# Seven chained products for the hidden layer, spread around the residual units, and one masking operation for two

## The reference

```python
h = jnp.maximum(_layernorm(x, axis=-1), 0.0)
x = x + _L0_gnn_ref(h, adj, adj, L0_gnn_W1, L0_gnn_W2, L0_gnn_W3)
h = jnp.maximum(_layernorm(x, axis=-1), 0.0)
x = x + _L1_gnn_ref(h, adj, L1_gnn_W1, L1_gnn_b1, L1_gnn_W2, L1_gnn_b2)
```

## Time and profile before

| | |
|---|---|
| median of 3 runs | 2262.76 us (2262.43 to 2263.21) |
| profiled execution | 2262.78 us, its span 2261.1 us |
| PE matmul busy | 2238.3 us, 99% |
| DVE busy | 1932.7 us, 85% |
| ACT busy | 1151.1 us, 51% |
| POOL busy | 1159.6 us, 51% |
| granted TensorE clock | 1.00 |

### The profile page before, as it was taken

One profiled execution on the slowest core, in us unless ns is written; L12 is line 12 of the kernel. 1 busy time (PEld: TensorE's weight loads), 2 busy tenths in 40 slices (PEclk: granted clock), 3 DMA queues, 4 the chain that ended last, 5 costly groups with the idle time before them and its releaser, 6 DMA issues.

```text
span 2261.1 us, 47549 instructions
## 1 busy us (share of the span) xinstructions
PE 2238.3 (99%) x12586; PEld 1905.3 (84%) x12586; DVE 1932.7 (85%) x10818; ACT 1151.1 (51%) x2901; POOL 1159.6 (51%) x1889
## 2 busy tenths in 40 slices
PE   8999999999999999999999999999999999999999
PEld 5777888888888888888888888888888888889998
DVE  7999999999888888888777778989999997547776
ACT  5555555555555555555555544444444444344554
POOL 6455555545555555555555557544555554343332
PEclk9999999999999999999999999999999999999999
DMA  3000000000000000000000000000000001024443
GB/s 105 29 29 29 16 24 29 29 29 20 29 29 29 29 29 19 19 28 28 28 28 28 28 29 20 29 29 19 24 25 28 28 28 38 19 80 132 135 132 107
DMA packets 90031, 90.14 MB, mean 40 GB/s; under 512 B 5376, under 2 KB 89088, under 8 KB 89856
## 3 DMA queue, kind: packets, MB, share of 16 engines
q1 hardware_dynamic: 89856, 88.23, 12.2%
HBM read 54.66 MB, written 33.55 MB: 39 GB/s over the span
## 4 chain that ended last, share of the span: by engine, by line
PE 91%; DVE 7%; ACT 1%; issue 1%; POOL 0%; DVEq 0%; ACTq 0%; POOLq 0%
PE ps L1550 74%; PE ps L1740 10%; PE ps L1472 3%; PE ps L1750 1%; DVE A L961 1%; PE ps L1683 1%; DVE A L965 1%; ACT squares L709 1%; DVE prods L998 1%; DVE xrow_sb L970 1%; ACT root_s L711 0%; DVE ps L1013 0%; DVE sc L979 0%; DVE sc L982 0%; DVE qcol L984 0%
## 5 line engine op out<-in xcount | busy, mean ns | idle before, releaser
L501 POOL COPY Eb<-sc 128x1 f32<-128x1 f32 (+1 forms) x254 | 46.7, 184 | 451.6 <-DVE v L986 231.9
L1550 PE MATMUL ps<-agg2T,w 128*128 128x256 f32 x1024 | 239.2, 379 | 0.0
L1550 PE MATMUL ps<-hid2T,xin 128*128 128x256 f32 x1024 | 236.1, 379 | 0.7 <-ACT h2T L754 0.7
L1550 PE MATMUL ps<-weightT,hid 128*128 128x256 f32 x1024 | 236.7, 379 | 0.0
L1550 PE MATMUL ps<-w,aggT 128*128 128x512 f32 x512 | 231.7, 592 | 0.0
L1550 PEld LDWEIGHTS ps<-weightT,hid 128*128 128x128 f32 x1024 | 189.5, 191 | 36.7 <-issue 14.3
L1550 PEld LDWEIGHTS ps<-hid2T,xin 128*128 128x128 f32 x1024 | 189.0, 190 | 26.2 <-ACT h2T L754 1.1
L1550 PEld LDWEIGHTS ps<-agg2T,w 128*128 128x128 f32 x1024 | 188.5, 190 | 25.3
L754 ACT ACTIVATE hid2T<-ps 128x512 f32<-128x512 f32 x256 | 151.0, 590 | 94.9 <-PE ps L1550 92.9
L1166 DVE SCALAR_TENSOR_TENSOR ahead<-ps,ne,ahead 128x14 f32<-128x14 f32 (+1 forms) x1020 | 189.9, 228 | 0.0
L1163 DVE RECIPROCAL ps<-ahead 128x14 f32<-128x14 f32 (+1 forms) x1024 | 188.3, 230 | 0.1
(11 more groups left out here) (387 smaller groups left out, 6194.3 us busy)
## 6 DMA issues: line engine op xcount, KB each, us to landing
xl<-in_x_dram SPq DMA_DIRECT2D x64, 256.0 KB, 2.8
xr<-in_x_dram SPq DMA_DIRECT2D x64, 256.0 KB, 2.8
x_dram<-xr SPq DMA_DIRECT2D x64, 256.0 KB, 2.3
xin<-x_dram SPq DMA_DIRECT2D x64, 256.0 KB, 2.8
out_dram<-xin SPq DMA_DIRECT2D x64, 256.0 KB, 2.2
w<-in_L_gnn_W_dram SPq DMA_DIRECT2D x1, 2048.0 KB, 10.3
w<-in_L_gnn_W_dram SPq DMA_DIRECT2D x1, 1024.0 KB, 12.2
w<-in_L_gnn_W_dram SPq DMA_DIRECT2D x1, 512.0 KB, 5.2
```

The lines of the kernel that those rows point to most:

```text
L501: pool.tensor_copy(Eb[:, bass.ds(k, 1)], sc[:, 4:5])
L1550: ins = pe.matmul(dst, a, b, start=start, stop=stop, skip_group_check=plan_.units[i][0][0] in "PG")
```

## The change

The hidden layer is computed as seven products of 256-column blocks, H1 to H7, the two items of a pair being the two block rows: seven units of two matmuls instead of four units of two matmuls of 512 columns. They are made for the NEXT pair at the end of the list: H1 H5 H2 H6, res 0, H7 H3, res 1, H4. H6, H7 and H4 accumulate in the bank of H1, H3 in that of H5; the banks come from a table (`bank_of`), and a unit waits for the last eviction of its own bank (`emptied`). POOL makes four sums of the aggregated nodes (`sum_of_nodes`) and three additions of products (`add_hid`); ACT evicts seven blocks and applies three ReLUs (`finish_hid`). The second aggregation now takes its blocks in the order (0,0) (1,1) (0,1) (1,0), each waiting for its own ReLU, and all four W2 sums on POOL wait for the last of them. `add_x` moves from the end of a round to step 1 of the next. The first pair keeps the old form, inside its first step. In householder_two the mask is applied to both blocks by one operation that reads a copy of `below` in PSUM (`under`), and the row's head is no longer cleared; ACT's squares start one column later instead.

```diff
         def columns(k0):
 
-            return max(k0, P) if k0 + 1 >= P else k0
+            return max(k0, P) if k0 + 1 >= P else k0 + 1
...
-        def plan(next_agg):
-            units = [("hid", j, q) for j in range(2) for q in range(NB)]
-            units += [("agg2", j, q) for q in range(H1B // 2) for j in range(2)]
+        def plan(next_pair):
+            units = [("agg2", 0, 0), ("agg2", 1, 1), ("agg2", 0, 1), ("agg2", 1, 0)]
             units += [(p, half, 0) for p in ("P1", "P5", "P6", "P3", "P7", "P2", "P4") for half in range(2)]
-            units += [("agg", j, 0) for j in range(2)] * next_agg
+            units += [("agg", j, 0) for j in range(2)] * next_pair
             units += [(p, m, 0) for p in ("G1", "G2", "G6", "G5", "G7", "G3", "G4") for m in range(NB)]
-            units += [("res", j, 0) for j in range(2)]
+            units += [("H1", 0, 0), ("H5", 0, 0), ("H2", 0, 0), ("H6", 0, 0)] * next_pair + [("res", 0, 0)]
+            units += [("H7", 0, 0), ("H3", 0, 0)] * next_pair + [("res", 1, 0)] + [("H4", 0, 0)] * next_pair
...
+        BANK_OF = {"H1": 1, "H5": 3, "H2": 0, "H6": 1, "H7": 1, "H3": 3, "H4": 1, "agg": 1}
...
+        HID_ADDS = (("C11", "H1", "H2"), ("C22", "H5", "H7"), ("C12", "H6", "H3"))
...
+            def sum_of_nodes(pair, n):
+
+                a11, a12, a21, a22 = (aggT[:, j, f, :] for j in range(2) for f in range(2))
+                a, b, op = {1: (a21, a22, ALU.add), 2: (node_block(1), a11, ALU.subtract), 3: (a11, a21, ALU.subtract),
+                            4: (a12, node_block(2), ALU.subtract)}[n]
+                if n == 1:
+                    pool.wait_ge(evac, before(pair - 1) + FULL.at["agg", 1, 0] + 3)
+                if n in (2, 4):
+                    pool.wait_ge(node_sum, 4 * pair + n - 1)
+                pool.tensor_tensor(node_block(n), a, b, op).then_inc(node_sum, 1)
+
+            def add_hid(pair, n):
+
+                name, other, block_ = HID_ADDS[n]
+                pool.wait_ge(evac, before(pair - 1) + FULL.at[block_, 0, 0] + 3)
+                pool.tensor_tensor(hid_block(name), hid_kept(other), hid_block(name), ALU.add).then_inc(hid_added, 1)
...
-                pool.wait_ge(evac, before(pair) + FULL.at["agg2", 1, 0 if n == 1 else 1] + 3)
+                pool.wait_ge(evac, before(pair) + FULL.at["agg2", 1, 0] + 3)
...
+                    if s == 1 and not (isinstance(t, int) and t == 0):
+                        for j in range(2):
+                            add_x(t - 1, j)
                     for kind, n in pool_turns[s]:
                         in_turn(t, kind, n)
-                for j in range(2):
-                    add_x(t, j)
...
+            def finish_hid(pair, n):
+
+                act.wait_ge(hid_added, len(HID_ADDS) * (pair - 1) + n + 1)
+                block_ = hid_block(HID_ADDS[n][0])
+                act.activation(block_, block_, ACT.Relu).then_inc(hid_fin, 1)
...
                 dve.wait_ge(col_ready, k + 2)
-                for b in range(NB):
-                    ins = dve.tensor_scalar(x_next[:, b:b + 1], col[:, b:b + 1], below[:, b, here:here + 1], None, ALU.mult)
-                at(ins)
-                at(dve.memset(head, 0.0), HOUSE - 20)
+                at(dve.tensor_tensor(x_next, col[:, :], under[:, :, here], ALU.mult), HOUSE - 19)
...
+                pe.wait_ge(evac, 8 if first_hid else before(pair) + emptied(plan_, i) + 3)
+                if stage in ("H5", "H6", "H7", "H3"):
+                    pe.wait_ge(node_sum, 4 * (pair + 1) + {"H5": 1, "H6": 2, "H7": 3, "H3": 4}[stage])
+                if (stage, j, q) == ("agg2", 1, 0) and not first_hid:
+                    pe.wait_ge(evac, before(pair - 1) + FULL.at["H4", 0, 0] + 3)
+                elif stage == "agg2" and not first_hid:
+                    pe.wait_ge(hid_fin, len(HID_ADDS) * (pair - 1) + {(0, 0): 1, (1, 1): 2, (0, 1): 3}[j, q])
```

More of the change, by code:

```diff
@@ L410, in placed @@
             return early, late, pool_turns
-        for first, last, steps, _ in GROUPS:
-            assert last - first == 1 or steps % 2 == 0
+        for (first, last, steps, _), k0 in zip(GROUPS, FIRST_STEP):
+            assert last - first == 1 or steps % 2 == 0 and k0 + 1 >= P
         @block.sync
@@ L592, in in_turn @@
                     sum_of_moving(pair, n)
+                elif kind == "hid":
+                    add_hid(pair + 1, n)
+                elif kind == "nodes":
+                    sum_of_nodes(pair + 1, n)
                 elif kind == "add":
@@ L633, in _ @@
                 keep_reflector(k, NB - 1)
+            for j in range(2):
+                add_x(WITH_STEPS - 1, j)
             pool.memset(halves[:, :, :], 0.0).then_inc(halved, 1)
@@ L690, in ln2_scalars, with pair_sums @@
                 pool.tensor_tensor(rs[:, s, 3, :], rs[:, s, 2, :], coef[:, 3, :], ALU.mult).then_inc(ln2_p, 1)
-            for s in range(2):
-                ln2_scalars(0, s)
+            def pair_sums(pair, more, plan_=FULL):
+                for n in range(1, 5):
+                    sum_of_moving(pair, n)
+                if more:
+                    for j in range(2):
+                        ln_minus_mean(pair + 1, j)
+                    for j in range(2):
+                        ln_scale(pair + 1, j)
+                for kind, n in POOL_ORDER[4:]:
+                    if more or kind not in ("nodes", "hid"):
+                        in_turn(pair, kind, n, plan_)
+                    if not more and (kind, n) == ("left", len(LEFTS) - 1):
+                        for s in range(2):
+                            ln2_scalars(0, s)
+            with pool.Fori(WITH_STEPS, PAIRS - 1) as t:
+                pair_sums(t, True)
+                for j in range(2):
+                    add_x(t, j)
             pair_sums(PAIRS - 1, False, ENDING)
@@ L764, in event @@
                     evacuate(pair, n)
+                elif kind == "hidfin":
+                    finish_hid(pair + 1, n)
                 else:
@@ L783, in act_steps @@
                     step_root(first_step + s, columns(k0 + s))
+                    if isinstance(t, int) and t == 0 and s == 0:
+                        for n, (j, q) in enumerate(FIRST_HID):
+                            act.wait_ge(unit, 2 + n + 1)
+                            act.activation(hid[:, j, q, :], ring[bank_of(("hid", j, q))][:, :], ACT.Relu).then_inc(evac, 1)
                     for kind, n in early_events[s]:
@@ L846, in pair_body @@
                         finish(pair, n)
+                    if more and (stage, j) in HID_AFTER:
+                        finish_hid(pair + 1, HID_AFTER[stage, j])
                     if more and (stage, j) == ("P2", 1):
@@ L851, in pair_body @@
                         act.activation(nrm[:, 1, :], nrm[:, 0, :], ACT.Sqrt).then_inc(z_root, 1)
-                    if not more and (stage, j, q) == ("agg2", 1, 1):
+                    if not more and (stage, j) == ("G5", 1):
                         normalise(0, 0)
```

157 lines of the change are left out of this document (101 added, 56 removed).

## The result

The changed kernel takes **2305.7 us** (median of 4 runs, 2304.96 to 2305.95) against 2262.6 before (4 runs beside them): 1.019 times as long, 95% interval 1.0177 to 1.0204, or 43 us slower.

The account below looks back on a forecast made before the run. PE, busy for 99% of the span, was taken to bound the kernel. Terms -25.8 - 6 + 30 + 10.5 + 14.5 + 2 = +25 us on 2262.76 gave 2288 us, range 2258 to 2305.

Parts of the forecast that it names:

- PE's own work: Matmuls of a pair: 28 records of 256 columns replace sixteen of 512, 0.83 us less for 31 pairs; -25.8 us.
- the rule of the narrow matmuls: Skill's issue gaps, estimated 98 ns for 256 columns, would make the change +66 us instead of -25.8; 2380 us, chance 0.01.
- The masking: DVE's Householder steps: one operation replaces two and a memset, 0.17 us off a late step; -6 us.
- POOL, added to and reordered: Step 2 of a round: PE waits for POOL's first sum, 1.7 us in early and 1.05 in 12-step rounds; +30 us.
- LayerNorm of the next pair: In 11-step rounds PE's aggregation waits for ACT's late LayerNorm output, 0.95 us for 11 rounds; +10.5 us.
- The end of a round on ACT: ACT's evictions and ReLUs delay the next round's root, so PE waits for q 0.9 or 0.5 us; +14.5 us.
- The rest: Rounds without steps: ACT and POOL wait for nothing of DVE, and evictions have time to spare; 0 us.
- The tail: Last pair: normalisation now stands behind one eviction and holds later ones; +2 us (0 to 4).
- rival 1 or 2: 1: everything hides as planned, 2233 us, chance 0.10; 2: only part of the waits comes true, 2262 us, chance 0.06.
- Rival 3: POOL, late by four sums in step 1, is late again, another 0.7 us in 22 rounds; 2303 us, chance 0.07.
- Rival 4: DVE is held by POOL's added operations, 4.4 us in each of 22 rounds; 2385 us, chance 0.01.

Follow-up runs that it names:

- the mended kernel: Changed kernel with five edits of order on POOL and ACT, plus first-round sums of weights ahead of LayerNorm's mean; 2229.2 us, 0.985 of the kernel before.
- LayerNorm one step earlier: Changed kernel with LayerNorm of the next pair placed one step earlier (LN_AT 0 and 1 in place of 1 and 2); 2285.2 us.
- Round 0: Changed kernel, first round only: POOL makes all eight weight sums in step 0, w3 sums in steps 2 and 3, w1 sums in step 6; 2300.3 us.

## Why the prediction was right or wrong

The sum came out 18 us too low (+25 against +43). Of that 10.9 us are the first round without steps, 5.0 are q in step 5, 4.3 are q in round 0, 2.4 and 2.1 the waits for POOL's sum and for LayerNorm, which were a little longer than forecast; against it stand 6.0 at the end of a round, which was forecast too long, and about 1 of all else. Without that error in the other direction the forecast would have been 24 us too low.

- **PE's own work**, -25.8: 25.4 by the sums of the paces. In a round without steps the pace holds:

```profile
1690.05 7.07 PE L1656 MATMUL ps<-weightT,hid 128*128 128x256 f32 x32
1696.96 1.24 PE L1656 MATMUL ps<-agg2T,w 128*128 128x256 f32 x5
```

  32 records in 1696.96 - 1690.05 = 6.91 us, 0.216 each, and such rounds are 56.54 us long, 0.82 shorter than before. By the rule of the narrow matmuls in the Trainium skill, "TensorE: Matmul & The Clock Gate", section "Back-to-back issue gap", these records would have taken more than half the time of wide ones; the trace doesn't show it. (The 98 ns of the forecast's estimate lie a third of the way between the two figures, by columns, not halfway.)
- **The masking**, -6: the sign right, the size too small. The operation saved 0.24 us a step, not 0.17: I took DVE's v row of 0.21 for it, and it took 0.15. On the kernel before it is worth 7.6, on the mended one 10.8. In the changed kernel its worth can't be told from the rest: rounds with steps also carry lateness behind the new waits.
- **POOL, added to and reordered**, +30: place, mechanism and size right. 1.8 us where I had 1.7, and 1.0 to 1.5 where I had 1.05 (0.5 in the last round); 32.4 us in all with round 0, and 30.0 came back when two additions moved.
- **LayerNorm of the next pair**, +10.5: right where I looked, 12.7 (1.6 us in round 0, then 1.3 falling to 0.86; I had 0.95 on average). The half I did not look at was POOL's. Its scale stands in step 4 ahead of the first addition of products; with everything on PE moved forward by the hidden layer, that addition became urgent, and cost 5.0 us in step 5.
- **The end of a round on ACT**, +14.5: the mechanism right, the size too large: 8.5 us of q and up to 1.6 in DVE's lateness after it. The root started 2.1 us in, as forecast (2.2), but PE's wait for q was 0.4 to 0.7, not 0.9, and 0.13 to 0.25, not 0.5. I had taken q's usual moment and added the lateness of the root; measured, q was 0.2 to 0.5 us less late than that.
- **The rest**, "In rounds without steps ACT and POOL wait for nothing of DVE", put at 0 in the sum: **this is the step that failed.** True of DVE, but in the first of those rounds PE waits for POOL's own preparation of the joins. That was 9.2 + 2.7 us where 1.0 had been, 11 of the 18 us by which the sum came out too low. It stood in the trace of before as a wait of 0.73 to 0.89 us, the only one of its kind, and I took it for closed because it was short. A wait in that place says that there is no slack; moving 6.9 us of work out from ahead of it makes it 6.9 us longer, and POOL came to its preparation 1 us later (1.17 us behind PE's first (tmp, ones) record before, 2.24 after). In the same way I had let the sums of w3 in round 0 stand where they were; together with LayerNorm's scale they cost 4.4 us of q there, of which 1.0 is left with both moved.
- **The tail**, +2: not seen at that size. The last pair has one new wait, 0.5 us for ACT's eviction of g (at 2041.55), and all rounds behind the first without steps together wait 1 us less than before.
- **The rivals.** Not rival 1 or 2. Rival 3 has nearly the measured time, but not the cause: no second wait followed the first in the 22 rounds. It came for one round and for a step that I had not followed. Rival 4 is excluded: POOL is busy 203 us longer, and in the rounds with steps DVE's 508 updates of A (A<-ps,A, of the same sizes in both kernels) take 0.415 us on average before and after; the mended kernel, with the same POOL work, takes 2229 us. DVE's 1020 operations of the earlier trace rows, behind those rounds, have their time too:

```profile
L1264 DVE SCALAR_TENSOR_TENSOR ahead<-ps,ne,ahead 128x14 f32<-128x14 f32 (+1 forms) x1020 | 189.6, 228 | 0.0
```

What stays open: why the half clock behind the same wait costs 1.1 to 1.7 us in some runs and 2.7 in others. The trace shows where they differ: in the changed kernel the clock is 0.50 from 4.7 us into the wait to 6.1 us after PE has gone on, with LayerNorm one step earlier from 5.1 us into it to 3.1 us after. Why it lasts longer in one than in the other isn't shown, so a gain of 1 to 2 us can't be credited to an edit.

## What to carry to other kernels

When work is moved out from ahead of a point, everything that was ready in time there is now asked for earlier by the whole length of that work, once for each place where the order is different: list those places (first round, last round, the seam between phases), and in each go through what stands in order ahead of the thing asked for, on every engine that takes part. A short wait in the trace of before can be the place with no slack, as it was here. And if an engine has the same work and only another order, mend the order before giving up the change: here 76 us lay in six moves.

## What was not expected of the hardware

- After PE had stood for 8.65 us, the granted clock was 0.50 from 1450 to 1456 us and 1.00 behind that; after a wait of 5.33 us in another kernel it was 0.79 on average of 14 us. The rounds with waits of 1.8 us kept 1.00 (100 to 160 us). The Trainium skill, "TensorE: Matmul & The Clock Gate", section "What's actually happening", says that an idle array falls to its lower clock; the trace agrees. The length of a wait alone doesn't settle it: behind one of 2.45 us in round 0 the clock was 0.50 (59.5 to 62.9 us, the run "Round 0"), behind one of 2.65 us at the same place it stayed at 1.00 (55 to 70 us, the run "LayerNorm one step earlier"). The forecast had no term for it, since it had no wait of that length.
- The masking, a TENSOR_TENSOR of 2 columns with one operand and the result in PSUM, took 0.15 us; the SCALAR_TENSOR_TENSOR of the same 2 columns that I had taken for its like takes 0.21.
- The reason that a row names for the end of a wait can be an engine that was done long before (0.73 us put down to ACT's h2T, above), and "issue" can stand for a wait of PE on POOL: times of ends on the other engine's timeline settle it.
